# Four of the eight moves of each q issued by GpSimd, and the projection weights issued ahead

## What is computed

```
x = x + attention(layernorm(x))      # 32 query heads, 8 key/value heads of 64, rotary embedding, causal softmax, Wo
x = x + ssm(ctx, z = layernorm(x))   # projection 128 -> 256, conv of 4 taps, silu, 16 states per channel, times silu(z)
x = x + ffn(layernorm(x))            # gate, up, down with a hidden width of 704, quantised int32 weights
```

```
q = (h @ Wq.T).reshape(b, s, 32, 64);  q = q * cos + rotate_half(q) * sin
logits = q k^T / 8, masked;  attn = softmax(logits);  out = attn v;  out @ Wo.T
```

## Time and profile before

| what | value |
|---|---|
| median of three runs | 546.08 us |
| the profiled execution's own time | 547.53 us |
| its span | 545.7 us |
| TensorE busy | 419.2 us, 77% |
| VectorE busy | 366.1 us, 67% |
| ScalarE busy | 272.0 us, 50% |
| GpSimd busy | 154.5 us, 28% |
| granted TensorE clock, mean | 0.891 of full speed |

### The profile page before, as it was taken

How to read it: one execution, slowest core, us unless ns; L and a number is a source line. 1 busy time by engine, 2 the same in 40 slices (tenths; PEclk the granted TensorE clock), 3 DMA queues, 4 the chain that set the end, 5 groups by cost and what they waited for, 6 DMA issues and landing times.

```text
span 545.7 us, 7590 instructions
## 1 busy us (share of the span) xinstructions
PE 419.2 (77%) x2604; PEld 328.9 (60%) x2636; DVE 366.1 (67%) x485; ACT 272.0 (50%) x779; POOL 154.5 (28%) x106
## 2 busy tenths in 40 slices
PE   3729480936869599696988979978998895459996
PEld 1523360725656477585777768857886783336774
DVE  2863232437898987589778848859785899855542
ACT  2214733506637465463667647647555575423321
POOL 2620000000263525133433423522242353311000
PEclk9867876868878989799999979999999998769999
DMA  8323213842134223230422233142113320000000
GB/s 201 64 65 94 52 30 72 225 125 84 35 96 132 81 94 86 74 97 19 129 76 58 50 115 97 32 136 92 29 37 121 97 69 29 0 1 13 21 21 25
DMA packets 53157, 40.62 MB, mean 74 GB/s; under 512 B 32280, under 2 KB 47840, under 8 KB 53120
## 3 DMA queue, kind: packets, MB, share of 16 engines
q1 hardware_dynamic: 51232, 39.21, 26.5%
q10 hardware_dynamic: 1888, 0.94, 0.6%
HBM read 26.36 MB, written 1.18 MB: 50 GB/s over the span
## 4 chain that ended last, share of the span: by engine, by line
PE 33%; SPq 18%; DVE 18%; issue 15%; DMA 7%; POOL 6%; ACT 3%; DVEq 0%; POOLq 0%
SPq L286 6%; PE ps_p L1015 6%; PE ps_s L1027 6%; SPq L297 5%; PE ps_p L1229 4%; POOL rc L411 4%; DVE state L780 4%; PE ps_s L1214 4%; PE ps_p L1127 3%; DVE nmax L698 3%; DMA qt<-rc 3%; DVE state L773 3%; PE ps_r L1081 2%; PE ps_o L1109 2%; DMA kt<-rc 2%
## 5 line engine op out<-in xcount | busy, mean ns | idle before, releaser
L483 ACT ACTIVATE prob<-ps_s,nmax 128x256 f32<-128x256 f32 (+1 forms) x256 | 104.8, 444 | 77.6 <-DVE nmax L698 77.6
L417 POOL TENSOR_TENSOR y<-y,state 128x1024 f32<-128x1024 f32 x32 | 80.4, 2512 | 167.1 <-DVE state L786 167.1
L411 POOL TENSOR_TENSOR rc<-rc,rs 128x512 f32<-128x512 f32 x40 | 57.2, 1431 | 150.4 <-DVE rs L686 104.3
L1015 PE MATMUL ps_p<-xt_all,wq 128*128 128x256 f32 x256 | 74.2, 440 | 28.8 <-DMA wq<-wqkv_t 20.4
L698 DVE TENSOR_REDUCE nmax<-ps_s 128x2 f32<-128x512 f32 (+1 forms) x96 | 60.3, 683 | 53.3 <-PE ps_s L1038 53.3
L489 ACT ACTIVATE pt<-ps_r 128x512 f32<-128x512 f32 x96 | 53.9, 593 | 77.4 <-PE ps_r L1081 73.8
L1027 PE MATMUL ps_s<-kt,qt 64*128 64x256 f32 (+1 forms) x512 | 57.2, 368 | 36.2 <-DMA qt<-rc 36.2
L780 DVE TENSOR_TENSOR_SCAN state<-decay,state 128x1024 f32<-128x1024 f32 x32 | 81.5, 2546 | 2.3 <-ACT decay L509 1.2
L1015 PEld LDWEIGHTS ps_p<-xt_all,wq 128*128 128x128 f32 x256 | 53.0, 217 | 43.5 <-issue 25.5
L1027 PEld LDWEIGHTS ps_s<-kt,qt 64*128 64x128 f32 x512 | 48.6, 207 | 44.1 <-DMA qt<-rc 38.2
L1127 PE MATMUL ps_p<-wo,attn_t 128*128 128x256 f32 x256 | 62.3, 391 | 8.0 <-DVE x L803 4.1
(11 more groups left out here) (109 smaller groups left out, 508.8 us busy)
## 6 DMA issues: line engine op xcount, KB each, us to landing
bc<-bc_scratch SPq DMA_DIRECT2D x32, 512.0 KB, 4.8
qt<-rc SPq DMA_DIRECT2D x256, 32.0 KB, 1.8
wq<-wqkv_t SPq DMA_DIRECT2D x32, 64.0 KB, 2.5
kt<-rc SPq DMA_DIRECT2D x64, 32.0 KB, 1.8
kt<-kt SPq DMA_DIRECT2D x8, 256.0 KB, 3.0
wo<-wo_t SPq DMA_DIRECT2D x1, 2048.0 KB, 9.3
xs<-x SPq DMA_DIRECT2D x1, 1024.0 KB, 7.6
out<-x SPq DMA_DIRECT2D x4, 256.0 KB, 2.1
```

The lines of the kernel that those rows point to most:

```text
L411: nc.gpsimd.tensor_tensor(rc[:, r % 2, :, :], rc[:, r % 2, :, :], rs[:], ALU.add).then_inc(rope_add, 1)
L417: nc.gpsimd.tensor_tensor(y[:, v % 2, :], y[:, v % 2, :], state[:, v % 2, :], ALU.add).then_inc(state_free, 1)
L483: nc.scalar.activation(o, i, ACT.Exp, bias=nmax[:, r, c:c + 1], accum_out=rsum[:, r, GRP + head:GRP + head + 1]).then_inc(exp_done, 1)
L1015: last = nc.tensor.matmul(o, lhs, rhs, start=(k == 0), stop=(k == KT - 1))
```

## The change

All eight moves of a q still exist. Heads 0 and 1 (four moves) stay with SyncE and count on a new semaphore pair `q_low`; heads 2 and 3 are issued by GpSimd, directly behind its own addition for that q, and count on `q_in`. TensorE's `scores` and VectorE's `rope` wait for both. wq 2 and 3 are issued by ScalarE's queue at the start, wk 1, wq 4 and 5 by SyncE after `move_q(1)`, and wq 6 and 7 by SyncE after `move_q(2)`. The loads of `wo` and of the feed-forward weights stay behind `move_k(1)` and ahead of `move_q(4)`.

```diff
+        def load_wq(queue, g):
+                for k in range(KT):
+                    for c in range(2):
+                        queue.dma_start(wq[:, k, g, c, :].rearrange("p (h i) -> p h i", i=HALF), w_q[k, g, c]
+                                        ).then_inc(wq_in[g], 16)
+        half_moves = q_moves // 2
+        q_low = [sem(f"q_low{r}") for r in range(2)]
+        def move_heads(queue, u, heads, landed):
+            r = ROPE_AT["q", u]
+            queue.wait_ge(rope_add, r + 1)
+            if u >= 2:
+                queue.wait_ge(score_done, 3 * (u - 1))
+            for h in heads:
+                for c in range(2):
+                    to = (h % 2) * HD + c * HALF
+                    queue.dma_start(qt[to:to + HALF, u % 2, h // 2, :], rc[h * HALF:(h + 1) * HALF, r % 2, c, :]
+                                    ).then_inc(landed[u % 2], 16)
...
@@ sync, at the start
-                load_wq(2)
@@ sync, move_q(u)
-                for h in range(GRP):
...
+                move_heads(sp, u, range(GRP // 2), q_low)
@@ sync
             move_q(1)
+                load_wk(1)
+            load_wq(sp, 4)
+            load_wq(sp, 5)
             sp.wait_ge(xdbl_sb, 2)
...
             move_q(2)
-                load_wk(1)
-                load_wq(3)
+            load_wq(sp, 6)
+            load_wq(sp, 7)
             move_q(3)
             move_k(1)
-                for g in range(4, KVH):
-                    load_wq(g)
             sp.dma_start(wo[:], ...
@@ gpsimd
             add_rope(("q", 0))
+            move_heads(nc.gpsimd, 0, range(GRP // 2, GRP), q_in)
             add_rope(("q", 1))
+            move_heads(nc.gpsimd, 1, range(GRP // 2, GRP), q_in)
...
                     add_rope(("q", u + 2))
+                    move_heads(nc.gpsimd, u + 2, range(GRP // 2, GRP), q_in)
@@ scalar, after its own loads and ahead of its first instruction
+            load_wq(nc.scalar, 2)
+            load_wq(nc.scalar, 3)
@@ vector, rope
-                        dve.wait_ge(q_in[i % 2], 16 * q_moves * (i // 2 + 1))
+                        dve.wait_ge(q_low[i % 2], 16 * half_moves * (i // 2 + 1))
+                        dve.wait_ge(q_in[i % 2], 16 * half_moves * (i // 2 + 1))
@@ tensor, scores
-                pe.wait_ge(q_in[r], 16 * q_moves * (u // 2 + 1))
+                pe.wait_ge(q_low[r], 16 * half_moves * (u // 2 + 1))
+                pe.wait_ge(q_in[r], 16 * half_moves * (u // 2 + 1))
```

More of the change, by code:

```diff
@@ L240, in decoder_layer @@
         x2lo_done = sem("x2lo_done")
-        q_moves, k_moves = 2 * GRP, 2 * KG
+        w_k = wqkv_t[:, :, GRP * HD:(GRP + 1) * HD].rearrange("(k p) (j g) (two i) -> k j two p g i", k=KT, j=2, two=2)
+        w_q = wqkv_t[:, :, 0:GRP * HD].rearrange("(k p) g (h two i) -> k g two p h i", k=KT, two=2, i=HALF)
+        def load_wq(queue, g):
+            with nc.allow_non_contiguous_dma(reason="weights by the halves of a head, once"):
+                for k in range(KT):
+                    for c in range(2):
+                        queue.dma_start(wq[:, k, g, c, :].rearrange("p (h i) -> p h i", i=HALF), w_q[k, g, c]
+                                        ).then_inc(wq_in[g], 16)
+        q_moves, k_moves = 2 * GRP, 2 * KG
+        half_moves = q_moves // 2
[10 more added lines that the diff above has]
+                                    ).then_inc(landed[u % 2], 16)
         block = ctx.enter_context(nc.Block())
@@ L259, in load_wk @@
                                          ).then_inc(wk_in[j], 16)
[L261 to L265, removed]
                 load_wk(0)
-                load_wq(0)
-                load_wq(1)
+                load_wq(sp, 0)
+                load_wq(sp, 1)
                 for k in range(KT):
@@ L315, in _ @@
             move_q(2)
-            with nc.allow_non_contiguous_dma(reason="weights by the halves of a head, once"):
-                load_wk(1)
-                load_wq(3)
+            load_wq(sp, 6)
+            load_wq(sp, 7)
             move_q(3)
             move_k(1)
-            with nc.allow_non_contiguous_dma(reason="weights by the halves of a head, once"):
-                for g in range(4, KVH):
-                    load_wq(g)
             sp.dma_start(wo[:], wo_t.rearrange("(k p) n -> p k n", p=P)).then_inc(wo_in, 16)
```

## The result

The changed kernel takes 524.02 us (median of four runs, 521.73 to 525.61) where the kernel before took 546.61 in the same comparison: ratio 0.9583, 95% interval 0.9539 to 0.9627. The forecast was 509, with 501 to 532 as its range. The direction was right and the gain was 60% of the one forecast: 22.6 us instead of 37.8. The profiled execution took 523.78 us, its span is 522.0.

A forecast was written before the change was run, and what follows sets the result against it. It took waits to bound the kernel, TensorE's 57 us for moves of q and wq, set by SyncE's order. Terms +1.6-2.5-20.6-13.7-3.6+1 = -37.8 us gave 509; own ends 503 to 517, range 501 to 532.

The forecast's parts named there:

- GpSimd's half last: Rival at the q moves: GpSimd's half lands after SyncE's, so the split gains little at boundaries; 529 us, chance 0.14.
- the dear start: Rival at the start: ScalarE's eight issues cost 2 us each, +10 us instead of +1.6; 518 us, chance 0.07.
- the other waits for q: Sign in the profile: TensorE's waits for q, besides those at the first scores and unit 4, under 2 us each.
- Step 1: At the start, wq 2 and 3 on ScalarE's queue delay its table load and GpSimd's first rstd: +1.6 us.
- Step 2: At the first scores, SyncE's half of the moves is done four issues earlier: -2.5 us.
- The price p: Cost of issuing one move on GpSimd, shown in no row; taken as 1.1 us.
- GpSimd the bound: Rival from unit 4 on: GpSimd's issues make it the bound from p = 1.8, up to 584 us; chance 0.09.
- The variant: Variant of GpSimd's half last: transfer, not issuing, sets landing, so splitting brings nothing at any p; 531 us, chance 0.03.
- Step 3: Up to the scores of unit 4, weights loaded ahead and SyncE's half of q 4 shorter: -20.6 us.
- Step 4: At later boundaries, four SyncE moves instead of eight shorten six waits for q: -13.7 us, and -3.6 by the clock.
- The clock's part: At later boundaries, the sixteen products behind three long waits run faster once remaining waits are below 2.76 us: -3.6 us.
- Step 5: At each scores and rope, one wait more: +1 us.

The follow-up runs named there:

- best_split: Changed kernel with bc loads behind the next q's moves, feed-forward loads behind those of q 4 and q 5, wq 2 and 3 on SyncE at the start: 490.93 us.
- bc_ffn: Changed kernel with the edits of bc_behind and ffn_late together: 494.52 us, ratio 0.9066.
- start_sp: Changed kernel with wq 2 and 3 issued by SyncE at the start instead of ScalarE: 521.48 us, ratio 0.9572.
- half_only: Changed kernel with only the split of the moves, all weights loaded as in the kernel before: 533.87 us, ratio 0.9793.
- all_pool: Changed kernel with all eight moves of a q on GpSimd and none on SyncE: 499.68 us, ratio 0.9164.
- ffn_late: Changed kernel with gate and down weights loaded behind the moves of q 4, wo and scales behind those of q 5: 511.39 us, ratio 0.9375.
- bc_behind: Changed kernel with a boundary's two bc loads issued by SyncE behind the next q's four moves instead of ahead: 505.63 us, ratio 0.9294.
- bc_act: Changed kernel with the boundaries' bc loads issued by ScalarE's queue at about the time of SyncE's q moves: 521.91 us, ratio 0.9576.
- before_bc_behind: Kernel before with only a boundary's two bc loads issued behind the next q's eight moves: 537.07 us, ratio 0.9864.
- weights_only: Changed kernel with only the weights moved ahead, all eight moves of a q left on SyncE: 533.49 us, ratio 0.9787.

## Why the prediction was right, and where it missed

The direction, the way in which the sum is built and the price of GpSimd's queue came out; the size did not. The measured 524 lies above the 503 to 517 that the forecast gave for its own ends. It is inside the stated 501 to 532 only because that range took in the 529 of a rival, GpSimd's half last, which did not come; the dear start ended at 518. That the range holds is in this sense luck. Of its signs, the other waits for q were to stay under 2 us each; three of them are 2.90, 2.93 and 3.19.

**Step 1, forecast +1.6, measured +3.6** (`best_split` against `bc_ffn`). The price per issue was right: 7.28 us for eight, 0.91 each against 0.93. Two things were missing. ScalarE's own loads before them got slower too (the first weight load starts at 5.58; the table load it displaced had been at 4.62). And VectorE's normalisation, behind the later rstd, took 5.72 us for eight instructions (4.60 before, 4.30 in `start_sp`). It goes with how far the two overlap: GpSimd's convolution starts 1.61, 0.91, 0.33 and 0.06 us behind it in `half_only`, `start_sp`, the kernel before and the changed kernel, and it takes 2.97, 4.30, 4.60 and 5.72 us. No run changes this overlap alone, so that the two hold each other up is likely, not shown.

**Step 2, forecast -2.5**: 3.0 in `half_only`, where nothing else moves the start. **The price p**, forecast 1.1, is 0.50. The two rivals that hang on it, GpSimd's half last and GpSimd the bound, are both refuted: in the changed kernel GpSimd's half at the boundary above is there by 293.0, before SyncE issues its own, and `all_pool` doubles GpSimd's load and is 24 us faster. The variant, that splitting brings nothing at any p, is refuted by `half_only`.

**Step 3, forecast -20.6, together with steps 1 and 2 -21.5; measured -16.1.** Its form held: the chain ends in SyncE's order, and ScalarE's copy of the probabilities (now at 70.17) still stands right behind prepare_scan(0). The terms were off. The addition of the k of group 1 came 5.1 us earlier, or 6.1 counted from the first scores, which were 1.05 later. That is the lower of the two ends named, not the midpoint of 7.8. The loads ahead of the moves of q 4 took 13.8 us instead of 12.2, and the start was 1.95 us worse: 1.7 + 1.6 + 1.95 = 5.3 of the 5.4 missing. The prediction called these loads what is late next and priced their issuing; `ffn_late` shows that 12.9 us of the kernel hung on their place.

**Step 4 is the step that failed: forecast -13.7 and -3.6 by the clock, measured -7.6 in all.** Of the 7.6, 5.7 are shorter waits (17.7 to 12.0 us) and 1.4 quicker products behind them. The prediction took SyncE's half to land in the time of the last of eight, 1.8 us by its median and 1.9 at this boundary. It did not ask when that last one was issued: 4.4 us after the bc loads, when these had nearly landed. Four moves less bring the deciding one forward into the bc transfer, and what was saved in issuing, 2.5 us, came back, at the boundary shown, as 2.2 us of landing; the wait there fell by 0.3 us, from 3.25 to 2.93. `bc_behind`, `bc_act` and `before_bc_behind` show this from three sides. The clock's part went with it: the remaining waits of 2.9, 2.9 and 3.2 us are still followed by products that take 1.74, 2.55 and 2.70 us, at a granted clock of 0.87, 0.60 and 0.57. The prediction read from four rows that only waits above 2.76 us are followed by slow products. The length of the wait alone does not tell it: in `weights_only` they take 1.58 us at 1.00 behind a wait of 3.48, in `bc_act` 2.25 at 0.68 behind one of 1.95.

**Step 5, +1**, can't be told apart from the rest. The rule of the Trainium skill that stood beside step 2 ("DMA: Bandwidth & Descriptors", "Issuing engines are not separate DMA queues") says in the same place that the DMAs of all issuing engines run on the same engines and interleave. The prediction weighed only its second half, on what issuing saves, and there the runs are against it: `half_only` gains 11 us by splitting the issuing alone. The first half agrees with `bc_act`, where moves of SyncE take 3.7 to 5.0 us beside loads of ScalarE's queue, and it points at the failed step.

## What to carry to other kernels

When the issuing of a group of DMAs is split or cut, ask what is on its way at the moment when the new last one goes out: a landing time read from the last of a long group can be that of a quiet moment. A half that sits in a queue behind other loads is still the whole wait, so look at the order of the queue that keeps a half as well (here 524 to 491 us, by two changes of order and by giving two weight loads back to SyncE). Loads put on a compute engine's queue hold up the first instruction of that engine for as long as their issuing takes; ScalarE's queue looked free at the start and cost 3.6 us.

## What was not expected of the hardware

- In the changed kernel GpSimd issues a 32 x 256 float32 move in 0.50 us (128 of them, 496 to 737 ns), less than SyncE's 0.59 with the 0.04 between two, and it lands in 1.7 us (median) against SyncE's 2.0, or 1.8 in the kernel before.
- A 32 KB move takes 3.7 to 5.0 us to land while two loads of 512 KB issued by another engine are on their way (`bc_act`), and 1.8 to 2.5 without them (`bc_behind`).
- The issue of the gate weights on SyncE takes 3.25 us behind the 2 MB load of wo (2.23 in the kernel before), and 0.58 in `ffn_late`, `bc_ffn` and `best_split`, where wo comes later.
